# From the seventh pair on, the values' first four products move from the second step of their slot to the fourth

## What is computed

```
x: (8, 1024, 256)
a = layernorm(x)
q, k, v = Wq a, Wk a, Wv a              # 16 heads of width 16
score   = q k^T / 4, causal, softmax, times v, then Wo
x = x + layernorm(that)
h = layernorm(x)
two of eight experts per token: (up + 1) * gate * sigmoid(1.702 gate), down_proj, weighted sum
x = x + layernorm(that)
```

## Time and profile before

| what | value |
| --- | --- |
| median of 3 runs | 2074.18 us (2072.88 to 2075.02) |
| the profiled execution, its own time | 2074.88 us |
| its span, first to last instruction | 2073.2 us |
| mean granted PE clock | 0.978 of full speed |
| PE busy | 1955.0 us, 94% |
| DVE busy | 1590.2 us, 77% |
| ACT busy | 1335.2 us, 64% |
| POOL busy | 938.9 us, 45% |

### The profile page before, as it was taken

One profiled execution on the slowest core, in us unless ns is written; L12 is line 12 of the kernel. 1 busy time (PEld: TensorE's weight loads), 2 busy tenths in 40 slices (PEclk: granted clock), 3 DMA queues, 4 the chain that ended last, 5 costly groups with the idle time before them and its releaser, 6 DMA issues.

```text
span 2073.2 us, 50254 instructions
## 1 busy us (share of the span) xinstructions
PE 1955.0 (94%) x13588; PEld 1294.9 (62%) x13589; DVE 1590.2 (77%) x5423; ACT 1335.2 (64%) x3405; POOL 938.9 (45%) x1439
## 2 busy tenths in 40 slices
PE   6899999999999999999999889999999999999990
PEld 5334444444444444444433338999999999999980
DVE  3877788888888888888787846878777777777777
ACT  4277777777777777777777675555444544544446
POOL 4333344455555646556454554554333333333336
PEclk9799999999999999999999999999999999999995
DMA  7633546465454554644536457988988889898878
GB/s 209 191 113 126 180 150 209 137 190 175 147 175 143 165 164 139 190 134 150 168 119 198 146 173 219 272 247 246 273 250 263 263 255 270 258 260 254 231 225 327
DMA packets 259188, 414.81 MB, mean 200 GB/s; under 512 B 37040, under 2 KB 194992, under 8 KB 251824
## 3 DMA queue, kind: packets, MB, share of 16 engines
q1 hardware_dynamic: 219520, 368.19, 54.9%
q0 software_dynamic: 29680, 35.41, 9.5%
q10 hardware_dynamic: 9792, 8.93, 1.4%
HBM read 289.55 MB, written 122.28 MB: 199 GB/s over the span
## 4 chain that ended last, share of the span: by engine, by line
PE 84%; DVE 8%; issue 4%; ACT 2%; POOL 1%; DMA 1%; DVEq 0%; SPq 0%; ACTq 0%; POOLq 0%
PE ps_s L1488 17%; PE ps_o L1372 13%; PE ps_s L1334 12%; PE ps_e L1353 10%; PE ps_e L1488 6%; PE ps_e L1505 5%; PE ps_o L1505 5%; PE ps_w L1404 5%; PE ps_w L1419 3%; PE ps_w L1435 3%; DVE arena L759 2%; PE ps_e L1498 1%; DVE cmax L762 1%; PE ps_w L1459 1%; DVE space L127 1%
## 5 line engine op out<-in xcount | busy, mean ns | idle before, releaser
L1127 ACT ACTIVATE arena<-ps_e 128x512 f32<-128x512 f32 (+3 forms) x1536 | 687.3, 493 | 276.7 <-PE ps_e L1353 263.3
L759 DVE CUSTOM_DVE_ANT_0 arena<-ps_s,c 128x128 bf16<-128x128 f32 (+3 forms) x1024 | 479.4, 481 | 67.3 <-PE ps_s L1334 63.5
L1334 PE MATMUL ps_s<-arena 96*128 96x512 bf16 (+3 forms) x1536 | 491.5, 335 | 20.4 <-DVE cmax L762 6.2
L1353 PE MATMUL ps_e<-arena 98*128 98x512 bf16 (+3 forms) x1536 | 482.9, 328 | 3.5 <-ACT arena L1127 2.3
L762 DVE TENSOR_REDUCE cmax<-ps_s 128x1 f32<-128x512 f32 x512 | 351.4, 686 | 143.8 <-PE ps_s L1334 134.1
L1334 PEld LDWEIGHTS ps_s<-arena 96*128 96x128 bf16 x1536 | 152.1, 101 | 354.5 <-DVE cmax L759 91.1
L1372 PE MATMUL ps_o<-arena 128*32 128x512 f32 (+3 forms) x3072 | 329.7, 501 | 6.3 <-ACT ot L1141 3.8
L655 POOL TENSOR_SCALAR_AFFINE_SELECT arena<-arena 128x512 f32<-128x512 f32 x256 | 163.6, 639 | 294.5 <-ACT arena L1127 294.2
L1488 PE MATMUL ps_s<-arena 128*128 128x128 f32 x2192 | 268.1, 275 | 0.4 <-issue 0.4
L638 POOL DMA_INDIRECT acc<-blank,place_now x135 | 212.2, 1572 | 123.2 <-POOL place_now L633 68.1
L1488 PEld LDWEIGHTS ps_s<-arena 128*128 128x128 f32 x2192 | 262.0, 192 | 6.2 <-issue 1.4
(11 more groups left out here) (187 smaller groups left out, 3048.2 us busy)
## 6 DMA issues: line engine op xcount, KB each, us to landing
arena<-in_gate_up SPq DMA_DIRECT2D x93, 1024.0 KB
arena<-qk_parts SPq DMA_DIRECT2D x384, 128.0 KB, 3.0
c_h<-in_gate_up SPq DMA_DIRECT2D x46, 1024.0 KB
qk_parts<-space SPq DMA_DIRECT2D x120, 192.0 KB
d_xin<-xs SPq DMA_DIRECT2D x140, 130.5 KB
arena<-v_aug SPq DMA_DIRECT2D x32, 512.0 KB
o_t<-ot SPq DMA_DIRECT2D x64, 256.0 KB, 2.0
v_aug<-space SPq DMA_DIRECT2D x28, 512.0 KB, 4.8
```

Of the source, the lines that this page charges most:

```text
L759: dve.tensor_tensor_reduce(summed[:, m % RJ, 0:w], ps_s[:, m % RS, 0:w], after[:, HALF - w:HALF], 1.0, LOWEST, ALU.add, ALU.max, dst).then ...
L1127: act.activation(pw[:, n % RP, 0:w], ps_e[:, n % RE, 0:w], ACT.Exp, scale=SCALE).then_inc(e_done, 1)
L1334: pe.matmul(ps_s[:, m % RS, 0:w], qs[0:ROWS, slot, i * P:(i + 1) * P], ks[0:ROWS, slot, k0:k0 + w], start=True, stop=True).then_inc(s_scor ...
L1353: pe.matmul(ps_e[:, n % RE, 0:w], ks[0:ROWS_M, slot, j * P:(j + 1) * P], qs[0:ROWS_M, slot, q0:q0 + w], start=True, stop=True).then_inc(e_ ...
```

## The change

For pairs 0 to 5 `values(a, 0)` stays where it was. For the pairs from 6 on it moves, in the same slot, from the second step (behind that step's two score products) to the fourth step (behind that step's score products and ahead of `weigh`). The waits in front of it are the same, its products are the same, and `values(a, 1)` stays in the second step of the next slot.

```
--- before.py
+++ after.py
@@ -1535,7 +1535,7 @@
                             q_or_k(a, 1, (2, 3))
                         for a in due(V_AT, 0, g):
                             values(a, 1)
-                        for a in due(V_AT, -1, g):
+                        for a in due(V_AT[0:EARLY + 2], -1, g):
                             values(a, 0)
                         for r in due(C_AT, 0, g):
                             project(r, 0)
@@ -1552,6 +1552,9 @@
                             q_or_k(a, 1, (0,))
                         for r in rows_due(15, 16, 16, g):
                             route(r, 0)
+                    if s == 3:
+                        for a in due(V_AT[EARLY + 2:], -1, g):
+                            values(EARLY + 2 + a, 0)
                 if g == NE * (QUADS - 1) + 9:
                     pe.wait_ge(s_cmax, HEADS * NM)
                     pe.wait_ge(rows_sb, HEADS)
```

## The result

The changed kernel takes 2085.18 us (median of 5 runs, 2083.76 to 2086.33), the kernel before 2074.18 us in the same session (2072.88 to 2075.59). The ratio is 1.0049, with a 95% interval of 1.0039 to 1.006. That is 11.0 us slower, where 10.5 us was forecast.

What follows compares the result with a forecast made beforehand. PE was taken as the bound; moved values would make it wait for DVE's maxima, 21 x 0.43 + 5 x 0.30 = 10.5 us more, on the median of 2074.18 giving 2084.7 us, range 2079 to 2092 us.

Steps and rivals of the forecast that it cites:

- The bound: Whole kernel: PE, busy 94% of the span against DVE's 77%, is the engine to follow.
- What PE can do at once: Slot 1: with the values moved away, PE does the third step's two score products inside the old wait, nothing more.
- the old wait: PE's wait at the values' products for DVE's remainder: 0.91 us once, then 25 times 0.45 us, 12.2 us in all.
- Where it stops: Slot 1, fourth step: score product and transposition wait for DVE's two maxima; transposition at 538.05, about 1.0 us idle.
- The terms: Transposition to slot 2: 0.15, values 0.92, product to `weigh` 0.21, `weigh` 1.00 us; late quads lose 0.43, early 0.30.
- The disputed 0.10 us: Ahead of `weigh`: its late start behind its waits was kept as surviving behind the values; without it losses are 0.33 and 0.20.
- The sum: All changed places: 21 late quads x 0.43 + 5 early quads x 0.30 = 10.5 us slower.
- Nothing given back: After slot 1: DVE, ACT and POOL hang on PE's scores, so none of the loss is recovered later.
- The hidden wait: Rival, slot 1: all 26 waits go and nothing takes their place, 12.2 us faster, 2062 us; 7%.
- The equal trade: Rival, slot 1 or behind it: the wait moves and costs the same, 2074 us, half absorbed 2072 to 2078; 9%.
- The clock: Rival, PE's new idle time: granted clock falls to half at least five times, 1.6 us each at most; 9%.
- Single falls: PE's clock at the changed place: one to three falls, up to 4.8 us, counted in the main range.

Runs made afterwards that it cites:

- second experiment: Changed kernel, with DVE's remainder of pairs 6 to 31 moved behind the maximum of slot 1's second step; 2075.57 us, ratio 1.0004 to the kernel before.
- fourth: Changed kernel, with DVE's two bn_aggr of quads 5 to 25 moved behind the second step's maximum; 2084.3 us, ratio 1.0042.
- first: Changed kernel, with the values' first four products of pairs 6 to 31 at the end of the third step instead; 2065.21 us, ratio 0.9952 to the kernel before.
- fifth experiment: Kernel before, values still in the second step, with DVE's remainder of pairs 6 to 31 behind the second step's maximum of slot 1; 2097.87 us, ratio 1.0114.
- seventh experiment: Changed kernel, with the values' first four products of pairs 6 to 31 directly behind line 1372 instead of ahead of it; 2087.88 us, ratio 1.0063.

## Why the prediction was right

**The bound.** PE was the engine to follow. Its busy time did not change by more than 0.5 us, and 9.4 of the 10.3 us of longer span are idle PE at 26 places, as the timeline of the changed kernel and the two stretches show.

**What PE can do at once.** The third step's two products fit into the old wait. The second of them did wait for ACT until 540.33, as the step allowed for, without consequence.

**Where it stops.** The product of the fourth step waits for line 762, 0.79 us late and 0.66 us early. The experiments confirm that place from three sides: the loss vanishes when the maxima come ahead of the remainder (second experiment), shrinks by what is taken out of DVE's queue (fourth), and turns into a gain when the values start ahead of it (first). I had put the idle time at about 1.0 us, some 26 us in all, on lines 1334 and 1341; the table of waits gained 20.1 us, all on line 1334. The transposition starts 0.30 us behind its score product where it took 0.20 before (538.34 to 538.54), so it does wait, for about 0.1 us, but the table does not book it.

**The terms.** In a late quad, forecast against measured: reading out to transposition 0.14 and 0.16 us; transposition to score product 0.15 and 0.14; from there through the values to line 1372, 1.13 and 1.08 (0.12 + 0.96); line 1372 to slot 2, 1.00 and 1.00. Slot 2 was forecast at 4.04 and came at 4.00 us. **The disputed 0.10 us** is the term that was mis-sized: with it the way from the last score product through the values to line 1372 would take 1.13 us, without it 1.03, and it takes 1.08. About half of it survives, 0.04 us of that in the values themselves (0.96 against 0.92 us). The rule of the Trainium skill, page "TensorE: Matmul & The Clock Gate", section "Architectural detail: the array is 16× 32×32, not 1× 128×128", by which weight loads are pulled ahead, gave 7.9 us, which is 1.5 us below the 9.4 us measured at the place, where my 10.5 lies 1.1 above. No run shows line 1372's load going ahead by more than 0.04 us: in the changed kernel too it starts together with its product, at 542.92. For the values the trace agrees: their first load starts at 541.85, their first product at 541.96.

**The sum.** 21 x 0.39 + 5 x 0.25 = 9.4 us by the measured distances, not 10.5. The median moved by 11.0 us. The 1.6 us between are not explained by the change, and the interval of the ratio, 8.1 to 12.4 us, covers both. In the profiled executions, which differ by 10.3 us, 1.2 us lie behind the last changed place, where the spread between kernels is of that size. So the forecast was within 0.5 us of the median partly by luck, and the mechanism itself was put 1.1 us too high: 0.04 us in each late quad and 0.05 in each early one.

**Nothing given back.** The period grew by exactly what slot 1 lost, 0.39 us.

**The rivals.** The hidden wait (2062 us) did not come, because the maxima were late by the microsecond or so that was worked out. But one step earlier, where I did not look, the same mechanism gives 2065 us. The equal trade did not happen. One reading in that rival was wrong: I called 6.2 us the next entry of PE's table of waits, and the next is 12.0 us, in a line that stands between the two shown in rows 2:

```profile
PE ps_e L1385 <- ACT space L1235: 12.0, 3, 10.4
```

These three waits lie ahead of the first changed place, the last of them ending at 26.3 us, so they could not have absorbed the loss. The clock did not fall in the changed kernel: it is 1.00 in quad 0 and over the whole stretch, with 0.79 us of idle PE in each late quad. Single falls, which the prediction had put into its main range, do occur at this place: in two of the experiments the clock fell once, in quad 0, and cost 1.5 and 1.6 us, about the price that I had put on one fall.

## What to carry to other kernels

A wait in the way of an engine may be the cover of others: before moving work out of a wait, list what that work hides, here two maxima behind the remainder in DVE's queue, and compare which result comes first. Here the best place for the block that must wait for the remainder and hides the maxima was the one at which the remainder had only just come and the maxima were not yet needed; one step too far costs more (0.72 us per quad from third to fourth) than the whole move could gain (0.33). When a program repeats to 0.01 us, its period decides questions that medians with a spread of 2 to 3 us cannot.

## What was not expected

- The four 128x256 float32 products cost PE 0.92 us from start to start between two score products, 0.97 us when they start behind a wait or behind line 1372, and 0.96 us ahead of line 1372 or of the transposition. In the second experiment, with line 1374 behind them, they cost 1.06 us, which is not explained. Line 1372 and the transposition both start 0.20 to 0.21 us behind a 256-column score product even when they wait for nothing, and another score product 0.11 us; directly behind the values only about 0.04 us of the difference remain.
- The lag from DVE to PE was 0.05 to 0.06 us from the end of line 782 or line 762, but 0.14 to 0.16 us from the end of the reading out that belongs to line 759 to the transposition. The reading out is not what makes it longer: in quad 0 of the changed kernel the score product of the third step starts at 99.37, 0.06 us behind a reading out that ended at 99.31. What fits is the 0.1 us by which the transposition also starts later behind a score product.
- An idle time of 0.79 us on PE every 37 us did not lower the granted clock once in 25 periods, nor did 1.31 us in the fifth experiment. The stretch over the 25 periods of that experiment, at full clock (columns as above), and ahead of it one microsecond of its quad 0, at half:

```profile
104.05:1044.91 940.86, 901.74 (x6046) 432.47 (x6045) 746.70 (x2745) 703.60 (x1701) 462.14 (x821) 1.00 0.50 155
```

```profile
100.00:101.00 1.00, 1.00 (x4) 0.44 (x3) 0.00 (x0) 0.00 (x0) 0.00 (x0) 0.50 0.00 0
```

- Quad 0 is the weak place. The clock fell there after 1.63 us of waiting (fifth experiment), and it fell in the seventh experiment after a wait of 0.66 us, though the changed kernel has the same wait and the same order up to there and kept its full clock. Why one of the two fell is open. The profile shows one execution of each kernel, so how often it happens is not known.
